# Layer norm spread over the steps of a two-block feed-forward kernel, and half of the second block's tiles normalised on ScalarE

## The chip, the cores and the metric

The kernel runs on one core of a Trainium2 chip. The metric is the device time in microseconds (us), the median over the runs shown. A profile of one execution shows what each engine did: PE is TensorE (PEld its weight loads), DVE is VectorE, ACT is ScalarE, POOL is GpSimd, SP is SyncE, which issues the large DMAs.

## What is computed

1024 tokens of width 256, float32. Two residual blocks, each behind a layer norm without weights:

```python
def _layernorm(x, axis=-1, eps=1e-05):
    m = jnp.mean(x, axis=axis, keepdims=True)
    v = jnp.var(x, axis=axis, keepdims=True)
    return (x - m) / jnp.sqrt(v + eps)
...
# block 1: 4 experts, the expert of a token follows from its id
for e in range(E):
    g = jax.nn.silu(jnp.einsum('bsd,fd->bsf', hidden_states, Wg[e]))
    u = jnp.einsum('bsd,fd->bsf', hidden_states, Wu[e])
    y = jnp.einsum('bsf,df->bsd', g * u, Wd[e])
    out = jnp.where((expert_ids == e)[..., None], y, out)
...
# block 2: 8 experts, the best two by score, weighed by a softmax
for e in range(E):
    h = jax.nn.silu(jnp.einsum('btd,hd->bth', x, W1[e])) * jnp.einsum('btd,hd->bth', x, W2[e])
    y = y + w[..., e:e + 1] * jnp.einsum('bth,dh->btd', h, W3[e])
...
x = x + _L0_xattn_ref(_layernorm(x, axis=-1), itok_BxS_13_99985, ctx_2048, ctx_2048, ctx_2048)
x = x + _L0_ffn_ref(_layernorm(x, axis=-1), L0_ffn_Wg, L0_ffn_W1, L0_ffn_W2, L0_ffn_W3)
```

In block 1 the three weights are the same tensor, so gate and up product are one.

## The kernel before

The tokens are two halves of 512 (h = 0, 1), each of four tiles of 128 tokens. The experts' hidden rows are cut into chunks of 128: 8 chunks in block 1 (b = 0), 11 in block 2 (b = 1). A **step** q is one chunk for one half: q 0 to 7 are block 1 of half 0, 8 to 15 block 1 of half 1, 16 to 26 block 2 of half 0, 27 to 37 block 2 of half 1. Every float32 product is made of three matmuls in a reduced format, from a high part and a low part of each operand (`w_hi`, `w_lo`, `hT_hi`, `hT_lo`, `act_hi`, `act_lo`).

All engines run the same list of steps, each in its own order, and wait on semaphores only:

- TensorE (`up`, `down`): `up(q)`, the product with the tokens into a PSUM bank `z` (6 matmuls of 512 columns in block 1, 12 in block 2), then the stages of slot 0, then `down(q-3)` (12 matmuls of 256 columns into `y`), then the stages of slot 1. `down` waits for `act_lo` of its step; a later `up` waits for earlier `act` results.
- ScalarE: `silu(q)` from `z` (L380), then `act_hi(q-1)` (L352), then this step's stages, then `w_hi` of a weight piece (L327).
- GpSimd: in block 1 `gated` = silu x gate (L315), then `rstd` (L285, a power of -0.5), then `w_lo` of a weight piece (L275). In block 2 only the last two.
- VectorE: in block 2 `gated` (L528); `act_lo(q-1)` (L503); `act(q)` (L538); `w_lo` of three pieces of block 1 (L509); then this step's stages, in the order residual sum, statistics, normalise (L436), tokens_lo (L443), router.

A **stage** stands in the table `STAGES`, which has three entries, for three **ways**: the layer norm of block 1 for half 1 (way (0,1), steps counted from 0), that of block 2 for half 0 (way (1,0), counted from 8) and for half 1 (way (1,1), counted from 16). The chain of a way is: statistics on VectorE, `rstd` on GpSimd, `norm` (4 tiles of 128x256) on VectorE, eight transposes on TensorE (`transpose_tokens`, L585), `tokens_hi` (L336) on ScalarE, `tokens_lo` on VectorE. TensorE waits inside its queue for each tile of `norm` that is late. In block 2 the router's scores, the best two and the softmax follow, and their gates (`gate_rows`, L492) are transposed at the end of step 16 and 26. `SPLIT_AT` says in which step a weight piece is split into `w_hi` and `w_lo`. The pieces come by DMA through a ring of 5 buffers.

Of the kernel before, what the change touches and what calls it, by code (L numbers as in the profile page):

```python
# [37 lines left out]
P = 128  # L38
# [18 lines left out]
BUFFERS = 3  # L57

RING = 5

# [15 lines left out]
    "statistics": (None, 2, 3),  # L76
    "inverse_deviation": (1, 4, 5),
    "normalise": (1, 4, 4),
    "transpose_tokens": ((4, 0), (6, 0), (6, 1)),
    "tokens_hi": (4, 5, 6),  # L80
    "tokens_lo": (5, 5, 5),
    "scores": (None, (7, 0), (7, 0)),
# [11 lines left out]
SPLIT_AT = {c - 3: (0, c) for c in range(FIRST_PIECES, CHUNKS[0])}  # L94
SPLIT_AT |= {6 + 2 * c: (1, c) for c in range(4)}
SPLIT_AT |= {FIRST[1, 0] + c - 5: (1, c) for c in range(4, CHUNKS[1])}
# [20 lines left out]
def ffn_moe(nc, x, token_ids, weights1, weights2, router, consts, out):  # L117
# [4 lines left out]
    with ctx:  # L122
# [35 lines left out]
        var = sb("var", [P, TILES])  # L158
        rstd = sb("rstd", [P, TILES])
        minus_half = sb("minus_half", [P, TILES])  # L160
        score_part = sb("score_part", [P, HALF_TILES, EXPERTS2])
# [22 lines left out]
        var_done, rstd_done = sem("var_done"), sem("rstd_done")  # L184
        norm_done, norm_T = sem("norm_done"), sem("norm_T")
        hT_hi_done, hT_lo_done = sem("hT_hi_done"), sem("hT_lo_done")
        scored, score_rows_done, scores_T = sem("scored"), sem("score_rows_done"), sem("scores_T")
# [83 lines left out]
        def _(pool):  # L271
# [6 lines left out]
            def inverse_deviation(b, h):  # L278

                for part, (n, tiles) in enumerate(LN_PARTS):  # L280
                    if n == ln_no(b, h):
# [4 lines left out]
                            .then_inc(rstd_done, 1)  # L286


            nc.gpsimd.memset(minus_half[:], -0.5).then_inc(reached_done, 1)
# [15 lines left out]
            for q, (b, h, c) in enumerate(STEPS):  # L305
                if b == 0:
# [5 lines left out]
                    if c == 0:  # L312
# [3 lines left out]
                        .then_inc(gated_done, 1)  # L316
                for way in due("inverse_deviation", q):
                    inverse_deviation(*way)
                if q in SPLIT_AT and SPLIT_AT[q] not in VECTOR_LO:
# [3 lines left out]
        def _(act_e):  # L323
# [5 lines left out]
            def tokens_hi(b, h):  # L329
                for k in range(KD):  # L330

                    act_e.wait_ge(norm_T, KD * ln_no(b, h) + k + 1)
                    if b == 1 and k == 0:

                        act_e.wait_ge(up_done, LAST[0, h] + 1)
                    nc.scalar.copy(hT_hi[:, h, k, :], y[h][k][:]).then_inc(hT_hi_done, 1)  # L336

            def gates_out(b, h):
# [35 lines left out]
            for q, (b, h, c) in enumerate(STEPS):  # L374
# [24 lines left out]
                if q in SPLIT_AT:  # L399
                    weight_hi(*SPLIT_AT[q])  # L400
            round_act(NSTEPS - 1)

        @block.vector
        def _(dve):
# [8 lines left out]
            def statistics(b, h, src):  # L413

                for n, tiles in LN_PARTS:
                    if n == ln_no(b, h):
# [8 lines left out]
                        link(last)  # L425
                        cols = slice(tiles.start, tiles.stop)
                        nc.vector.tensor_scalar(var[:, cols], mv[:, cols, 1], EPS, None, ALU.add).then_inc(var_done, 1)

            def normalise(b, h, src):
                if ln_no(b, h):  # L430

                    dve.wait_ge(norm_T, KD * ln_no(b, h))
                for i, t in enumerate(tiles_of(h)):

                    dve.wait_ge(rstd_done, ln_part_no(ln_no(b, h), t))
                    nc.vector.tensor_scalar(norm[:, i, :], src[:, t, :], mv[:, t, 0:1], rstd[:, t:t + 1],  # L436
                                            ALU.subtract, ALU.mult).then_inc(norm_done, 1)
# [82 lines left out]
            for q, (b, h, c) in enumerate(STEPS):  # L520
# [31 lines left out]
                for bb, hh in due("normalise", q):  # L552
                    normalise(bb, hh, (x_sb, x2_sb)[bb])
                for way in due("tokens_lo", q):
# [17 lines left out]
        def _(pe):  # L572
# [7 lines left out]
            def transpose_tokens(b, h):  # L580
                for k in range(KD):
                    for i in range(HALF_TILES):

                        pe.wait_ge(norm_done, HALF_TILES * ln_no(b, h) + i + 1)
                        last = nc.tensor.transpose(y[h][k][:, i * P:(i + 1) * P], norm[:, i, k * P:(k + 1) * P], ident)  # L585
# [146 lines left out]
```

## Time and profile before

| | us |
|---|---|
| median of 3 runs | 166.16 |
| the runs | 165.45, 166.16, 166.22 |
| span of the profiled execution | 165.1 |
| TensorE busy | 154.5 (94%) |
| VectorE busy | 114.8 (70%) |
| ScalarE busy | 65.1 (39%) |
| GpSimd busy | 55.9 (34%) |

TensorE is busy nearly throughout, so its remaining idle stretches, and the stretches in which its clock was granted at less than full speed, are where time is to be found. An engine's share of busy time includes time in which a running instruction was held up.

### The profile page before, as it was taken

The page shows a single profiled execution, that of the slowest core. Times are in us where ns is not written, and L with a number is a line of the kernel's source. Part 1 is how long each engine was busy: PE and PEld are TensorE (multiplying, and loading weights), DVE is VectorE, ACT ScalarE, POOL GpSimd, SP SyncE. Part 2 cuts the span into 40 slices and gives each one's busy share as a digit, 9 for nine tenths or more (in the row PEclk, how much of TensorE's full clock was granted, in tenths as well). Part 3 has the DMA queues.
Part 4 walks back from the last instruction along what each step waited for, and adds up shares of the span by engine and source line. Part 5 has one row for each costly group of instructions (what it writes and reads, how often), then busy time and mean ns, then how long its engine had stood idle before and what let it go on. Part 6 is the DMA issues. An engine that isn't in the chain of part 4 may idle for free.

```text
span 165.1 us, 2425 instructions
## 1 busy us (share of the span) xinstructions
PE 154.5 (94%) x892; PEld 131.7 (80%) x892; DVE 114.8 (70%) x225; ACT 65.1 (39%) x115; POOL 55.9 (34%) x47
## 2 busy tenths in 40 slices
PE   7599799999995999999999999999999999999991
PEld 2177689898982879888888778898888888888890
DVE  0788999955989865799999784945444744444452
ACT  3395557643742431763344432206222222222210
POOL 0599825779796330757464000000000000000000
PEclk9999999999999599999999999999999999999999
DMA  3975325232033000150000000000000300000003
GB/s 104 331 271 173 95 67 142 81 95 81 22 95 95 0 0 4 16 175 0 0 0 4 2 0 0 2 4 0 0 0 0 126 5 0 0 0 4 0 2 127
DMA packets 4332, 8.76 MB, mean 53 GB/s; under 512 B 736, under 2 KB 864, under 8 KB 4320
## 3 DMA queue, kind: packets, MB, share of 16 engines
q1 hardware_dynamic: 4176, 8.60, 16.7%
q8 instruction: 7, 0.11, 0.3%
q14 instruction: 5, 0.04, 0.1%
q10 hardware_dynamic: 144, 0.00, 0.0%
HBM read 7.55 MB, written 1.05 MB: 52 GB/s over the span
## 4 chain that ended last, share of the span: by engine, by line
PE 46%; DVE 17%; issue 14%; POOL 13%; ACT 4%; DMA 3%; SPq 1%; DVEq 0%; POOLq 0%; ACTq 0%
PE z L626 26%; PE y L651 18%; POOL gated L315 9%; DVE act L538 4%; DVE act_lo L503 4%; POOL w_lo L275 3%; DMA raw<-weights_dram 3%; DVE norm L436 2%; DVE x_sb L449 2%; DVE stats L421 2%; DVE gated L528 2%; ACT act_hi L352 1%; ACT w_hi L327 1%; PE y L585 1%; POOL rstd L285 1%
## 5 line engine op out<-in xcount | busy, mean ns | idle before, releaser
L626 PE MATMUL z<-hT_hi,w_hi 128*128 128x512 f32 x120 | 48.0, 400 | 0.6 <-ACT hT_hi L336 0.3
L626 PE MATMUL z<-hT_hi,w_lo 128*128 128x512 f32 x120 | 47.4, 395 | 0.0
L503 DVE TENSOR_TENSOR act_lo<-act,act_hi 128x512 fp32r<-128x512 f32 x38 | 33.4, 880 | 15.0 <-ACT act_hi L352 14.4
L651 PE MATMUL y<-w_hi,act_lo 128*128 128x256 f32 x152 | 43.5, 286 | 0.2 <-DVE act_lo L503 0.2
L651 PE MATMUL y<-w_hi,act_hi 128*128 128x256 f32 x152 | 43.5, 286 | 0.0
L651 PE MATMUL y<-w_lo,act_hi 128*128 128x256 f32 x152 | 43.4, 286 | 0.0
L380 ACT ACTIVATE silu<-z 128x512 f32<-128x512 f32 x38 | 22.7, 597 | 45.2 <-PE z L626 45.2
L626 PE MATMUL z<-hT_lo,w_hi 128*128 128x512 f32 x120 | 37.2, 391 | 0.0
L275 POOL TENSOR_TENSOR w_lo<-raw,w_hi 128x768 fp32r<-128x768 f32 (+1 forms) x15 | 27.4, 1839 | 19.3 <-ACT w_hi L327 19.3
L352 ACT CAST act_hi<-act 128x512 fp32r<-128x512 f32 x38 | 23.5, 618 | 26.0 <-DVE act L538 25.6
L651 PEld LDWEIGHTS y<-w_hi,act_lo 128*128 128x128 f32 x152 | 29.4, 193 | 2.1 <-issue 0.4
L651 PEld LDWEIGHTS y<-w_lo,act_hi 128*128 128x128 f32 x152 | 29.4, 194 | 1.2
L528 DVE TENSOR_TENSOR gated<-gate,z 128x512 f32<-128x512 f32 x22 | 15.0, 683 | 21.3 <-PE z L626 19.6
L651 PEld LDWEIGHTS y<-w_hi,act_hi 128*128 128x128 f32 x152 | 29.5, 194 | 0.0
L626 PEld LDWEIGHTS z<-hT_lo,w_hi 128*128 128x128 f32 x120 | 22.6, 188 | 5.3 <-DVE hT_lo L443 0.3
L626 PEld LDWEIGHTS z<-hT_hi,w_hi 128*128 128x128 f32 x120 | 22.9, 191 | 4.6 <-issue 0.9
L315 POOL TENSOR_TENSOR gated<-silu,gate 128x512 f32<-128x512 f32 x16 | 23.0, 1451 | 10.6 <-ACT silu L380 10.6
L626 PEld LDWEIGHTS z<-hT_hi,w_lo 128*128 128x128 f32 x120 | 22.9, 191 | 3.7
L538 DVE TENSOR_TENSOR act<-gated,silu 128x512 f32<-128x512 f32 x22 | 18.3, 833 | 0.0
L327 ACT CAST w_hi<-raw 128x768 fp32r<-128x768 f32 (+1 forms) x19 | 14.0, 742 | 4.4 <-DMA raw<-weights_dram 4.4
L538 DVE TENSOR_TENSOR act<-gated,z 128x512 f32<-128x512 f32 x16 | 10.9, 678 | 2.4 <-POOL gated L315 2.4
L436 DVE TENSOR_SCALAR norm<-x_sb,mv,rstd 128x256 f32<-128x256 f32 x16 | 10.4, 704 | 0.3 <-POOL rstd L285 0.3
(48 smaller groups left out, 75.3 us busy)
## 6 DMA issues: line engine op xcount, KB each, us to landing
raw<-weights_dram SPq DMA_DIRECT2D x11, 384.0 KB, 3.2
raw<-weights_dram SPq DMA_DIRECT2D x8, 256.0 KB, 4.8
x_sb<-x_dram SPq DMA_DIRECT2D x4, 256.0 KB, 4.6
out_dram<-x_sb SPq DMA_DIRECT2D x4, 256.0 KB, 2.5
consts_sb<-consts_dram SPq DMA_DIRECT2D x1, 68.0 KB, 3.8
ids_sb<-token_ids_dram ACTq DMA_DIRECT2D x1, 4.0 KB, 4.0
router_raw<-router_dram SPq DMA_DIRECT2D x1, 8.0 KB, 2.8
```

The costliest lines, as they stand in the source:

```text
L275: nc.gpsimd.tensor_tensor(w_lo[b][:, c, :], raw_piece(b, c), w_hi[b][:, c, :].bitcast(F32), ALU.subtract).then_inc(w_lo_pool, 1)
L315: nc.gpsimd.tensor_tensor(gated[:, q % BUFFERS, :], silu[:, q % BUFFERS, :], gate[:, h, :], ALU.mult)\
L327: nc.scalar.copy(w_hi[b][:, c, :], raw_piece(b, c)).then_inc(w_hi_done, 1)
L352: nc.scalar.copy(act_hi[:, q % BUFFERS, :], act[:, q % BUFFERS, :]).then_inc(act_hi_done, 1)
L380: nc.scalar.activation(silu[:, q % BUFFERS, :], z_banks(q)[0][:], ACT.Silu).then_inc(silu_done, 1)
L421: last = nc.vector.bn_stats(stats[:, t, :], src[:, t, :])
L436: nc.vector.tensor_scalar(norm[:, i, :], src[:, t, :], mv[:, t, 0:1], rstd[:, t:t + 1], ALU.subtract, ALU.mult).then_inc(norm_done, 1)
L503: nc.vector.tensor_tensor(act_lo[:, i, :], act[:, i, :], act_hi[:, i, :].bitcast(F32), ALU.subtract)\
L528: nc.vector.tensor_tensor(gated[:, i, :], gate[:, h, :], z_banks(q)[1][:], ALU.mult)\
L538: nc.vector.tensor_tensor(act[:, i, :], gated[:, i, :], factor, ALU.mult).then_inc(act_done, 1)
L626: return nc.tensor.matmul(bank[:], w[b][:, c, cols], tokens[:, h, k, :], **flags)
L651: last = nc.tensor.matmul(o, a[:, q % BUFFERS, rows], w[b][:, c, wd], start=(first and j == 0), stop=(c == CHUNKS[b] - 1 and j == 2), skip ...
```

## The change

Three things are changed.

- **Block 1, half 1.** The four `norm` tiles, which VectorE wrote one behind the other in step 1, are written one in each of the steps 1 to 4, each at the end of its step. The transposes move from slot 0 of step 4 to slot 0 of step 5, `tokens_hi` from step 4 to 5 and `tokens_lo` from step 5 to 6.
- **Block 2, half 0.** `rstd` and `norm` move from step 12 to step 11. `w_hi` and `w_lo` of piece (1,3) move from step 12 to step 14. The places of the other stages are as before.
- **Both halves of block 2.** VectorE writes two `norm` tiles; ScalarE writes the other two as `rstd * x + shift`. For that VectorE writes `minus_mean` (128x4) with the statistics, and GpSimd `shift = minus_mean * rstd` (128x2). In half 1 `rstd` moves from step 21 to 20; `norm` stays in step 20. ScalarE's two tiles come at the end of its step 11 (step 20 in half 1) and wait for `shift`.

```diff
@@ -56,6 +56,9 @@
 LAG = 3
 BUFFERS = 3
 
+
+DVE_TILES = 2
+
 RING = 5
 
 WARM = 12
@@ -74,11 +77,11 @@
 STAGES = {
     "sum": (None, 1, 2),
     "statistics": (None, 2, 3),
-    "inverse_deviation": (1, 4, 5),
-    "normalise": (1, 4, 4),
-    "transpose_tokens": ((4, 0), (6, 0), (6, 1)),
-    "tokens_hi": (4, 5, 6),
-    "tokens_lo": (5, 5, 5),
+    "inverse_deviation": (1, 3, 4),
+    "normalise": (None, 3, 4),
+    "transpose_tokens": ((5, 0), (6, 0), (6, 1)),
+    "tokens_hi": (5, 5, 6),
+    "tokens_lo": (6, 5, 5),
     "scores": (None, (7, 0), (7, 0)),
     "score_rows": (None, 7, 7),
     "transpose_scores": (None, (7, 1), (7, 1)),
@@ -92,7 +95,7 @@
 
 FIRST_PIECES = 4
 SPLIT_AT = {c - 3: (0, c) for c in range(FIRST_PIECES, CHUNKS[0])}
-SPLIT_AT |= {6 + 2 * c: (1, c) for c in range(4)}
+SPLIT_AT |= {(6, 8, 10, 14)[c]: (1, c) for c in range(4)}
 SPLIT_AT |= {FIRST[1, 0] + c - 5: (1, c) for c in range(4, CHUNKS[1])}
 
 VECTOR_LO = ((0, 0), (0, 5), (0, 6), (0, 7))
@@ -157,6 +160,8 @@
         mv = sb("mv", [P, TILES, 2])
         var = sb("var", [P, TILES])
         rstd = sb("rstd", [P, TILES])
+        shift = sb("shift", [P, TILES])
+        minus_mean = sb("minus_mean", [P, TILES])
         minus_half = sb("minus_half", [P, TILES])
         score_part = sb("score_part", [P, HALF_TILES, EXPERTS2])
         score = sb("score", [P, HALF_TILES, EXPERTS2])
@@ -183,6 +188,7 @@
         gate_T, gate_done = sem("gate_T"), sem("gate_done")
         var_done, rstd_done = sem("var_done"), sem("rstd_done")
         norm_done, norm_T = sem("norm_done"), sem("norm_T")
+        shift_done, norm_act = sem("shift_done"), sem("norm_act")
         hT_hi_done, hT_lo_done = sem("hT_hi_done"), sem("hT_lo_done")
         scored, score_rows_done, scores_T = sem("scored"), sem("score_rows_done"), sem("scores_T")
         gap_done, th_done = sem("gap_done"), sem("th_done")
@@ -285,6 +291,12 @@
                         nc.gpsimd.tensor_tensor(rstd[:, cols], var[:, cols], minus_half[:, cols], ALU.pow)\
                             .then_inc(rstd_done, 1)
 
+            def scaled_mean(h):
+
+                pool.wait_ge(rstd_done, ln_part_no(ln_no(1, h), h * HALF_TILES))
+                cols = slice(h * HALF_TILES + DVE_TILES, (h + 1) * HALF_TILES)
+                nc.gpsimd.tensor_tensor(shift[:, cols], minus_mean[:, cols], rstd[:, cols], ALU.mult).then_inc(shift_done, 1)
+
 
             nc.gpsimd.memset(minus_half[:], -0.5).then_inc(reached_done, 1)
             nc.gpsimd.memset(reached[:, 0, :], 1.0).then_inc(reached_done, 1)
@@ -314,8 +326,10 @@
                         pool.wait_ge(gate_done, ln_no(b, h) + 1)
                     nc.gpsimd.tensor_tensor(gated[:, q % BUFFERS, :], silu[:, q % BUFFERS, :], gate[:, h, :], ALU.mult)\
                         .then_inc(gated_done, 1)
-                for way in due("inverse_deviation", q):
-                    inverse_deviation(*way)
+                for bb, hh in due("inverse_deviation", q):
+                    inverse_deviation(bb, hh)
+                    if bb == 1:
+                        scaled_mean(hh)
                 if q in SPLIT_AT and SPLIT_AT[q] not in VECTOR_LO:
                     weight_lo(*SPLIT_AT[q])
 
@@ -334,6 +348,16 @@
 
                         act_e.wait_ge(up_done, LAST[0, h] + 1)
                     nc.scalar.copy(hT_hi[:, h, k, :], y[h][k][:]).then_inc(hT_hi_done, 1)
+
+            def normalise_rest(h):
+                act_e.wait_ge(shift_done, h + 1)
+                act_e.wait_ge(rstd_done, ln_part_no(ln_no(1, h), h * HALF_TILES))
+
+                act_e.wait_ge(norm_T, KD * ln_no(1, h))
+                for i in range(DVE_TILES, HALF_TILES):
+                    t = h * HALF_TILES + i
+                    nc.scalar.activation(norm[:, i, :], x2_sb[:, t, :], ACT.Identity, bias=shift[:, t:t + 1],
+                                         scale=rstd[:, t:t + 1]).then_inc(norm_act, 1)
 
             def gates_out(b, h):
 
@@ -398,6 +422,8 @@
                     gates_out(*way)
                 if q in SPLIT_AT:
                     weight_hi(*SPLIT_AT[q])
+                for _, hh in due("normalise", q):
+                    normalise_rest(hh)
             round_act(NSTEPS - 1)
 
         @block.vector
@@ -424,13 +450,15 @@
                             last = nc.vector.bn_aggr(mv[:, t, :], stats[:, t, :])
                         link(last)
                         cols = slice(tiles.start, tiles.stop)
+                        if b == 1:
+                            nc.vector.tensor_scalar(minus_mean[:, cols], mv[:, cols, 0], -1.0, None, ALU.mult)
                         nc.vector.tensor_scalar(var[:, cols], mv[:, cols, 1], EPS, None, ALU.add).then_inc(var_done, 1)
 
-            def normalise(b, h, src):
+            def normalise(b, h, src, parts=range(HALF_TILES)):
                 if ln_no(b, h):
 
                     dve.wait_ge(norm_T, KD * ln_no(b, h))
-                for i, t in enumerate(tiles_of(h)):
+                for i, t in [(i, h * HALF_TILES + i) for i in parts]:
 
                     dve.wait_ge(rstd_done, ln_part_no(ln_no(b, h), t))
                     nc.vector.tensor_scalar(norm[:, i, :], src[:, t, :], mv[:, t, 0:1], rstd[:, t:t + 1],
@@ -550,7 +578,10 @@
                     dve.wait_ge(x2_done, 2 * hh + 2)
                     statistics(1, hh, x2_sb)
                 for bb, hh in due("normalise", q):
-                    normalise(bb, hh, (x_sb, x2_sb)[bb])
+                    normalise(bb, hh, x2_sb, range(DVE_TILES))
+                if 1 <= q <= HALF_TILES:
+
+                    normalise(0, 1, x_sb, (q - 1,))
                 for way in due("tokens_lo", q):
                     tokens_lo(*way)
                 for _, hh in due("best_two", q):
@@ -581,7 +612,12 @@
                 for k in range(KD):
                     for i in range(HALF_TILES):
 
-                        pe.wait_ge(norm_done, HALF_TILES * ln_no(b, h) + i + 1)
+                        if b == 0:
+                            pe.wait_ge(norm_done, HALF_TILES * h + i + 1)
+                        elif i < DVE_TILES:
+                            pe.wait_ge(norm_done, 2 * HALF_TILES + DVE_TILES * h + i + 1)
+                        else:
+                            pe.wait_ge(norm_act, (HALF_TILES - DVE_TILES) * h + i - DVE_TILES + 1)
                         last = nc.tensor.transpose(y[h][k][:, i * P:(i + 1) * P], norm[:, i, k * P:(k + 1) * P], ident)
                     last.then_inc(norm_T, 1)
```

VectorE's queue, steps 1 to 4: `act_lo` (of the step before), `act`, `w_lo` (a weight piece) and `norm`. Before:

```order
L503 TENSOR_TENSOR act_lo<-act,act_hi 128x512 [waits act_hi_done]
L538 TENSOR_TENSOR act<-gated,z 128x512 [waits gated_done]
L436 TENSOR_SCALAR norm<-x_sb,mv,rstd 128x256 [waits rstd_done,norm_T]
L436 TENSOR_SCALAR norm<-x_sb,mv,rstd 128x256 [waits rstd_done] x3
L503 TENSOR_TENSOR act_lo<-act,act_hi 128x512 [waits act_hi_done]
L538 TENSOR_TENSOR act<-gated,z 128x512 [waits gated_done]
L509 TENSOR_TENSOR w_lo<-raw,w_hi 128x512 [waits w_hi_done]
```

And with the change, from the third of these `act_lo` on (steps 3 and 4):

```order
L531 TENSOR_TENSOR act_lo<-act,act_hi 128x512 [waits act_hi_done]
L566 TENSOR_TENSOR act<-gated,z 128x512 [waits gated_done]
L537 TENSOR_TENSOR w_lo<-raw,w_hi 128x512 [waits w_hi_done]
L464 TENSOR_SCALAR norm<-x_sb,mv,rstd 128x256 [waits rstd_done,norm_T]
L531 TENSOR_TENSOR act_lo<-act,act_hi 128x512 [waits down_done,act_hi_done]
L566 TENSOR_TENSOR act<-gated,z 128x512 [waits gated_done]
L537 TENSOR_TENSOR w_lo<-raw,w_hi 128x512 [waits w_hi_done]
L464 TENSOR_SCALAR norm<-x_sb,mv,rstd 128x256 [waits rstd_done,norm_T]
```

The last `norm` tile now stands behind nine other instructions of VectorE that it stood ahead of.

TensorE's queue, end of `up(5)` and the transposes of block 1's half 1, with the change (before, they stood behind `up(4)`, ahead of `down(1)`):

```order
L662 MATMUL z<-hT_hi,w_hi 128x512 [waits act_done,w_lo_vector]
L662 MATMUL z<-hT_hi,w_lo 128x512
L662 MATMUL z<-hT_hi,w_hi 128x512
L662 MATMUL z<-hT_hi,w_lo 128x512
L662 MATMUL z<-hT_lo,w_hi 128x512 x2
L621 MATMUL y<-consts_sb,norm 128x128 [waits norm_done,gate_done]
L621 MATMUL y<-consts_sb,norm 128x128 [waits norm_done] x7
L687 MATMUL y<-w_hi,act_lo 128x256 [waits act_lo_done]
```

They moved back by one `down` and one `up`: `down(2)` now stands behind them.

GpSimd's queue, steps 10 to 15. Before (`rstd` and `w_lo` of piece (1,3) are the fourth and fifth row):

```order
L315 TENSOR_TENSOR gated<-silu,gate 128x512 [waits act_done,silu_done] x2
L275 TENSOR_TENSOR w_lo<-raw,w_hi 128x768 [waits w_hi_done]
L315 TENSOR_TENSOR gated<-silu,gate 128x512 [waits act_done,silu_done] x2
L285 TENSOR_TENSOR rstd<-var,minus_half 128x4 [waits var_done]
L275 TENSOR_TENSOR w_lo<-raw,w_hi 128x768 [waits w_hi_done]
L315 TENSOR_TENSOR gated<-silu,gate 128x512 [waits act_done,silu_done] x3
```

And with the change:

```order
L281 TENSOR_TENSOR w_lo<-raw,w_hi 128x768 [waits w_hi_done]
L327 TENSOR_TENSOR gated<-silu,gate 128x512 [waits act_done,silu_done]
L291 TENSOR_TENSOR rstd<-var,minus_half 128x4 [waits var_done]
L298 TENSOR_TENSOR shift<-minus_mean,rstd 128x2 [waits rstd_done]
L327 TENSOR_TENSOR gated<-silu,gate 128x512 [waits act_done,silu_done] x3
L281 TENSOR_TENSOR w_lo<-raw,w_hi 128x768 [waits w_hi_done]
L327 TENSOR_TENSOR gated<-silu,gate 128x512 [waits act_done,silu_done]
```

`rstd` moved ahead of one `gated`, and `w_lo` of piece (1,3) from ahead of three `gated` to between the last two (those of steps 14 and 15).

## Rows read from the trace of the kernel before

**Rows 1.** The page: VectorE and others' busy time, and TensorE's granted clock in 40 slices
```profile
PE 154.5 (94%) x892; PEld 131.7 (80%) x892; DVE 114.8 (70%) x225; ACT 65.1 (39%) x115; POOL 55.9 (34%) x47
...
PEclk9999999999999599999999999999999999999999
```

**Rows 2.** Timeline, TensorE, step 4: start us, us busy, instruction, [idle before, releaser]
```profile
19.26 0.38 PE L585 MATMUL y<-consts_sb,norm 128*128 128x128 f32 x2
20.51 1.09 PE L585 MATMUL y<-consts_sb,norm 128*128 128x128 f32 x6 [0.88 <-DVE norm L436]
...
24.36 0.28 PE L651 MATMUL y<-w_hi,act_lo 128*128 128x256 f32 x1
```

**Rows 3.** Timeline, TensorE, the transposes of block 2's halves
```profile
51.03 0.30 PE L585 MATMUL y<-consts_sb,norm 128*128 128x128 f32 x1 [1.09 <-DVE norm L436]
52.21 1.41 PE L585 MATMUL y<-consts_sb,norm 128*128 128x128 f32 x7 [0.88 <-DVE norm L436]
53.38 0.36 PE L651 MATMUL y<-w_hi,act_lo 128*128 128x256 f32 x1
...
90.88 1.04 PE L585 MATMUL y<-consts_sb,norm 128*128 128x128 f32 x8
```

**Rows 4.** The chain that ended last, merged: start us, us, what
```profile
53.62 2.39 PE y L651 x12
56.02 1.96 PE z L626 x6
...
63.61 1.43 PE y L651 x12
...
111.16 2.75 PE z L626 x12
```

**Rows 5.** Timeline, VectorE, steps 1 to 4
```profile
16.73 4.05 DVE L436 TENSOR_SCALAR norm<-x_sb,mv,rstd 128x256 f32<-128x256 f32 x4
...
22.67 0.69 DVE L503 TENSOR_TENSOR act_lo<-act,act_hi 128x512 fp32r<-128x512 f32 x1
...
26.69 0.68 DVE L509 TENSOR_TENSOR w_lo<-raw,w_hi 128x512 fp32r<-128x512 f32 x1
```

**Rows 6.** Timeline, GpSimd, the same stretch
```profile
17.54 1.35 POOL L315 TENSOR_TENSOR gated<-silu,gate 128x512 f32<-128x512 f32 x1
19.04 1.26 POOL L315 TENSOR_TENSOR gated<-silu,gate 128x512 f32<-128x512 f32 x1 [0.15 <-ACT silu L380]
...
26.68 3.54 POOL L315 TENSOR_TENSOR gated<-silu,gate 128x512 f32<-128x512 f32 x2 [1.66 <-ACT silu L380]
```

**Rows 7.** Line L436 by stretch: ns min/median/max, starts (first and second tile, last)
```profile
L436 DVE TENSOR_SCALAR norm<-x_sb,mv,rstd x2: 1008/1196/1385, 16.7 to 17.7; 128x256 f32<-128x256 f32 x2
...
L436 DVE TENSOR_SCALAR norm<-x_sb,mv,rstd x1: 401/401/401, 20.4 to 20.4; 128x256 f32<-128x256 f32 x1
```

**Rows 8.** Timeline, GpSimd and VectorE side by side in block 2
```profile
79.53 1.85 POOL L275 TENSOR_TENSOR w_lo<-raw,w_hi 128x768 fp32r<-128x768 f32 x1 [2.02 <-ACT w_hi L327]
...
79.78 2.15 DVE L503 TENSOR_TENSOR act_lo<-act,act_hi 128x512 fp32r<-128x512 f32 x1
```

**Rows 9.** Groups by line, ScalarE: instruction xcount | busy us, mean ns | idle before
```profile
L352 ACT CAST act_hi<-act 128x512 fp32r<-128x512 f32 x38 | 23.5, 618 | 26.0 <-DVE act L538 25.6
...
L396 ACT ACTIVATE th<-gap 128x4 f32<-128x4 f32 x2 | 0.4, 205 | 6.2 <-DVE gap L471 6.2
```

**Rows 10.** Timeline, GpSimd, step 12 and step 15
```profile
47.92 1.00 POOL L285 TENSOR_TENSOR rstd<-var,minus_half 128x4 f32<-128x4 f32 x1
...
58.69 1.29 POOL L315 TENSOR_TENSOR gated<-silu,gate 128x512 f32<-128x512 f32 x1 [2.53 <-ACT silu L380]
```

**Rows 11.** Timeline, VectorE then TensorE, from act(15) to the gates' transposes
```profile
60.45 0.68 DVE L538 TENSOR_TENSOR act<-gated,z 128x512 f32<-128x512 f32 x1
...
63.91 0.63 DVE L492 COPY gate_rows<-w_tok 128x128 f32<-128x128 f32 x4
...
64.88 0.60 PE L577 MATMUL y<-consts_sb,gate_rows 128*128 128x128 f32 x4
```

## The prediction

> **What bounds the kernel now.** The page comes first: TensorE is busy 94% of the span, and in one of 40 slices, the fourteenth (53.7 to 57.8 us), its granted clock is about half [rows 1]. So the kernel gets shorter where TensorE waits or runs slowly, and nowhere else. The timeline of TensorE then gives the places. In step 4 it has done two transposes of block 1's half 1 when it waits 0.88 us for VectorE's `norm` [rows 2]. In step 14, at the transposes of block 2's half 0, it waits 1.09 and 0.88 us [rows 3]. The transposes of half 1 wait for nothing: eight take 1.04 us [rows 3]. The rest of the span is nearly free of idle time on TensorE but for the start and the end.
>
> What these places cost. Step 4: from the first transpose to the last 20.51 + 1.09 - 19.26 = 2.34, against 1.04: **1.3 us**. Step 14: TensorE came at 51.03 - 1.09 = 49.94, and was done at 52.21 + 1.41 = 53.62, against 50.98: 2.6, with the usual overlap of neighbours some **2.7 us**. Behind that idle stretch the clock fell to its lower level (1.2 GHz): `down(11)` took 2.39 us where the same 12 matmuls take 1.43, and the 6 of `up(15)` 1.96 where 12 take 2.75, so 6 about 1.38 [rows 4]. That is 0.96 + 0.58, some **1.6 us**. All three together are 5.6 us, 3.4% of the span.
>
> Why `norm` is late there: not by its own work. The last of the four tiles in step 1 took 0.40 us, the first 1.01 and the second 1.39 [rows 7]. The second started at 17.7 and ended at 19.05, just behind GpSimd's `gated`, 17.54 to 18.89 [rows 6]; four tiles took 4.05 [rows 5]. The same shows with two-input instructions of VectorE: `act_lo` started at 79.78 and ended at 81.93, while `w_lo` on GpSimd ran from 79.53 to 81.38, so it ended 0.55 behind it, where it takes 0.69 alone [rows 5, 8]. It goes the other way too: two `gated` took 3.54 against 1.26 for one [rows 6], 1.0 too much. So where an instruction of VectorE that reads SBUF twice (or a `norm` tile) meets one of GpSimd, the later one waits for the whole of the earlier.
> The Trainium skill (SBUF — State Buffer, "SBUF: two separate sides") says so of the pair of ports that the two engines share: an exclusive lock, held for the instruction. The trace agrees (2.15 us beside 1.85). If the two shared bandwidth instead, the walk below would be shorter by its held-up time and the sum would be that of the first rival.
>
> **The change, part by part.**
>
> *Block 1, half 1: one `norm` tile a step.* The first tile runs as before, 16.73 to 17.74. `down(1)` no longer stands behind the transposes, only behind `act_lo(1)`. That now meets `gated(2)` and ends at 18.89 + 0.55 = 19.44, so `down(1)` starts at 19.5, not at 21.4; `up(5)` waits a little for `w_lo` of piece 5 and is over at about 22.8. There the transposes stand, and they need the fourth tile. It stands behind `act_lo`, `act` and `w_lo` of steps 2 to 4: nine instructions of 0.6 us each from start to start (0.69 less the overlap) and three tiles of 0.33. Free of hold-ups the fourth tile would start at 16.73 + 9 x 0.60 + 3 x 0.33 = 23.1 and end at 23.5. Hold-ups, from the rows of the same pairs: first tile against `w_lo` 0.6; `act_lo(1)` against `gated(2)` 1.1; `w_lo` against `gated(3)` 0.8; against `gated(4)` 0.6; against `gated(5)` 0.7. Sum 3.8: the fourth tile ends at 27.3. A cross-check: before, the same 13 instructions in another order took from 16.73 to 26.69 + 0.68 = 27.37 [rows 5]. The total hardly changes, but the tile that TensorE needs was third from the front and is now the last.
> So TensorE comes at 22.8 and stands until 27.3, but for one transpose when the third tile comes (about 24.4); four or five more transposes take 0.6, and `down(2)` starts at 27.9 instead of 24.36 [rows 2]. This is net of the 1.3 us stall that goes: **+3.5 us**. Bounds: -0.2 (nothing held up: 23.5 + 0.6 against 24.36) and +4.2. I take 3.5, because the cross-check sits on it.
>
> *The clock there.* 4 us with three transposes is longer and emptier than the 3.1 us with one or two in step 14, behind which the clock fell [rows 3]. So it probably falls here. Price: 0 to 1.6, as in step 14; if it falls, **+1.3**, since part of the slow stretch can lie in the idle time itself.
>
> *Does the lateness last?* ScalarE's `tokens_hi` now stands in front of `silu(6)`, and waits for the transposes; `gated`, `w_lo` and `act` of steps 6 to 11 come some 1.5 us later than before, but TensorE comes 3.5 later, so it meets no new wait; it was continuously busy from step 5 to 13 and stays so. `tokens_lo` in step 6 is ready within half a microsecond of where `up(8)` needs it. Taken at nothing; at worst 0.5.
>
> *Block 2, half 0.* `rstd` ran at 47.92 to 48.92 [rows 10] and now runs one `gated` (1.3) earlier relative to its neighbours. With the lateness of 1.5 it ends near 48.7, `shift` (a 128x2 product) near 49.0, VectorE's two tiles near 49.5. ScalarE's two tiles are in no row; the 128x512 copies take 0.62 and a 128x4 0.2 [rows 9], so 0.2 to 0.6 each, I take 0.5 (near the larger, as they are long instructions): done near 50.1. TensorE comes at 49.8 + 3.5 = 53.3. Three microseconds of slack, so the wait goes and with it the fall of the clock: **-2.7 - 1.6 = -4.3 us**. It would have gone even with four tiles on VectorE. Of the 4.3 the bounds are 2.7 (the clock falls all the same) and 4.3.
> The Trainium skill (ScalarE: Activation LUTs, "What ACT_TABLE_LOAD costs") gives 186 ns, 93 more for each per-partition operand, and 0.833 ns an element: by it a tile would be an estimated 0.59 us. No row here shows it, and with 3 us of slack the sum stays the same.
>
> *`w_lo` of piece (1,3) between `gated(14)` and `gated(15)`.* Before, `gated(15)` ran at 58.69 as soon as silu was there [rows 10], `act(15)` at 60.45, and the gates' last row was ready at 64.54, just before TensorE wanted it at 64.88 [rows 11]. Now GpSimd is in `w_lo` (1.85 [rows 8], held up by `act_lo(13)` to 2.3) when silu(15) comes: it is free 1.5 later and held up again by `act_lo(14)` (0.5). In the new clock of events, without a fall of TensorE's clock, `act(15)` starts at 60.9, the gates' rows are ready 64.54 - 60.45 = 4.1 later at 65.0, and TensorE, which has gained, is there at 63.9 + 0.2: **+0.9 us**. Bounds 0 and 1.5.
>
> *Block 2, half 1.* `rstd` and `shift` go ahead of one `w_lo`, so VectorE's `var` is no longer held up, but that `w_lo` now meets `act` and the tiles, and ends where it did. The transposes waited for nothing before. Taken at nothing, bounds -0.4 and +0.4. The added `minus_mean`, 128x4, is under 0.1 and hidden by that slack; `shift` (twice) too.
>
> **Sum** against the profiled execution: 165.1 + 3.5 + 1.3 - 4.3 + 0.9 = 166.5. The median of the runs is 1.06 above the span, so **167.5 us**, +1.3.
>
> **The rivals.**
> 1. *The stall in step 5 is short.* The queues fall so that VectorE is seldom held up, the fourth tile is ready at 23.5 to 25.5, the clock stays up. For it: each hold-up depends on tenths of a microsecond. Against it: the cross-check. Time: 166.2 + (-0.2 to +1.7) - 4.3 + 0.9 = 162.6 to 164.5. Chance 0.18.
> 2. *The stall is as said, but the clock doesn't fall.* For it: the idle time of step 4 before, 0.9 us, brought no fall. Then 167.5 - 1.3 = 166.2 (165.4 to 166.7). Chance 0.25.
> 3. *Slower by more*, decided by whether the slow clock lasts on. If the clock falls in step 5 and again at the gates of step 16, where TensorE waits 0.9, or if the stretch at the lower clock is twice as long, 1.6 more: 169.0. It decides from the point where idle time at step 16 passes that of step 14 before. Chance 0.10.
> Forecast as said, 166.7 to 168.4: chance 0.47.
>
> **Range and chances.** 164.8 to 168.4: it leaves out rival 3 and the lower part of rival 1, 2 in 10. The forecast and rival 2 alone would give 165.4 to 168.4. A measurement of this kernel can tell 0.5% (0.83 us) from no change. Faster by more than that, under 165.33: all of rival 1 and a small part of 2, 0.20. Slower, over 166.99: most of the forecast's 0.47 and rival 3, 0.50. Between: 0.30.
>
> **What would show it.** In the changed kernel's timeline: the transposes of block 1's half 1 start near 22.8, with idle time before the last of them until about 27.3, and `down(2)` starts at 27.9. If they end before 25, rival 1 holds. The granted clock shows half in a slice near 26 to 32 us, or else rival 2 holds. The transposes in step 14 show no idle time before them and no half clock behind; if they do, the -4.3 is wrong. The gates' transposes in step 16 wait for `gate_rows` by about 0.9. I'd be wrong above all if VectorE's order of waiting and GpSimd's differ from the walk, since its five hold-ups carry the sum.

## The result: slower, 1.027 times

The changed kernel takes 170.87 us in the median of five runs, the kernel before 166.22 in its five: the ratio is 1.027, 95% interval 1.021 to 1.033. The forecast had the sign, 167.5 us, but the time lies outside the stated range of 164.8 to 168.4. The profiled execution has a span of 167.8 us and belongs to the run of 169.58; three of the other runs have spans of 169.0 to 169.1 and a lower mean clock (0.976 to 0.979 of full speed instead of 0.99). The fifth, 174.44 us at 0.959, is left out of the ratio, as every run is that lies over 1.5% above the fastest of its kernel. Time less span is 1.8 us in every run of every kernel whose span is known.

The page of the changed kernel, totals and granted clock, to be set beside [rows 1]:

```profile
PE 154.3 (92%) x892; PEld 131.4 (78%) x892; DVE 112.6 (67%) x223; ACT 67.1 (40%) x119; POOL 58.1 (35%) x49
...
PEclk9959999999999999999999999999999999999999
```

The slice with half clock is now the third, at the first transposes of the program, and no longer the fourteenth. The timeline of TensorE, at the places of the prediction (start us, us, instruction, [idle before, releaser]):

```profile
8.86 1.81 PE L621 MATMUL y<-consts_sb,norm 128*128 128x128 f32 x8
...
20.53 0.39 PE L687 MATMUL y<-w_hi,act_lo 128*128 128x256 f32 x1 [0.17 <-DVE act_lo L531]
...
23.72 0.38 PE L621 MATMUL y<-consts_sb,norm 128*128 128x128 f32 x2
25.18 0.33 PE L621 MATMUL y<-consts_sb,norm 128*128 128x128 f32 x1 [1.07 <-DVE norm L464]
27.77 0.77 PE L621 MATMUL y<-consts_sb,norm 128*128 128x128 f32 x5 [2.27 <-DVE norm L464]
28.30 0.36 PE L687 MATMUL y<-w_hi,act_lo 128*128 128x256 f32 x1
...
54.16 1.03 PE L621 MATMUL y<-consts_sb,norm 128*128 128x128 f32 x8
...
55.86 0.39 PE L687 MATMUL y<-w_hi,act_lo 128*128 128x256 f32 x1 [0.66 <-DVE act_lo L531]
...
59.63 0.64 PE L631 MATMUL y<-hT_hi,router_hl 128*16 128x512 f32 x2 [0.69 <-DVE hT_lo L471]
...
67.63 0.73 PE L608 MATMUL y<-consts_sb,gate_rows 128*128 128x128 f32 x4 [0.62 <-DVE gate_rows L520]
```

How to read it beside [rows 2, 3, 11]. The stall of step 4 (0.88 idle) has become one of 1.07 and 2.27 in step 5. The stall of step 14 is gone: eight transposes in 1.03, as half 1 had them before. Behind it stand three waits that were not there: `down(11)` for `act_lo`, the router's scores for `hT_lo`, the gates' transposes for `gate_rows`.

TensorE's groups come in the same order in both kernels but for the one that moved. The difference of their starts, changed kernel less the one before, shows where time comes and goes. The second column of numbers is from another execution of the changed kernel, `after_again`, told of below:

| TensorE's group | changed kernel | its other execution | what happened since the row above |
|---|---|---|---|
| `down(0)` | +0.95 | +0.02 | half clock at the first transposes, in one of the two |
| `down(2)` | +3.94 | +3.48 | the stall of step 5 |
| `down(4)` | +4.02 | +4.37 | half clock behind it, in the other of the two |
| `down(5)`, behind `up(8)` | +4.42 | +4.78 | `up(8)` waits 0.4 for `hT_lo` |
| `up(14)` | +4.38 | +4.75 | nothing in 15 us |
| `up(15)` | +1.58 | +1.94 | stall and half clock of step 14 gone, `down(11)` waits |
| scores of half 0 | +1.82 | +2.18 | wait for `hT_lo` |
| `down(13)` | +1.97 | +2.32 | |
| `up(17)` | +2.90 | +3.27 | wait for `gate_rows` |
| `up(22)` | +2.50 | +2.89 | the 0.22 us wait of before gone |
| scores of half 1, and on to the end | +2.69 | +3.08 | the tokens come no earlier |

### The profile page after: what moved, and what is told of

Its sections match the earlier page's. It is cut to its first block, busy times and chain, and to the rows that moved or that the text cites. A ratio compares the mean times of both kernels' runs of the same rounds, so it can differ in the third digit from the quotient of the medians.

```text
span 167.8 us, 2434 instructions
## 1 busy us (share of the span) xinstructions
PE 154.3 (92%) x892; PEld 131.4 (78%) x892; DVE 112.6 (67%) x223; ACT 67.1 (40%) x119; POOL 58.1 (35%) x49
## 3 DMA queue, kind: packets, MB, share of 16 engines
HBM read 7.55 MB, written 1.05 MB: 51 GB/s over the span
## 4 chain that ended last, share of the span: by engine, by line
PE 47%; DVE 29%; issue 8%; ACT 6%; POOL 4%; DMA 3%; SPq 1%; ACTq 0%; DVEq 0%; POOLq 0%
PE z L662 26%; PE y L687 18%; DVE act L566 8%; DVE act_lo L531 6%; DMA raw<-weights_dram 3%; DVE norm L464 2%; DVE stats L447 2%; ACT act_hi L376 2%; DVE w_lo L537 2%; DVE hT_lo L471 2%; POOL gated L327 2%; PE y L621 1%; POOL w_lo L281 1%; ACT hT_hi L350 1%; DVE x_sb L477 1%
## 5 line engine op out<-in xcount | busy, mean ns | idle before, releaser
L531 DVE TENSOR_TENSOR act_lo<-act,act_hi 128x512 fp32r<-128x512 f32 x38 | 34.5, 907 | 18.8 <-ACT act_hi L376 18.6
L687 PE MATMUL y<-w_hi,act_hi 128*128 128x256 f32 x152 | 43.0, 283 | 0.0
L281 POOL TENSOR_TENSOR w_lo<-raw,w_hi 128x768 fp32r<-128x768 f32 (+1 forms) x15 | 28.3, 1895 | 13.0 <-ACT w_hi L341 12.8
L687 PEld LDWEIGHTS y<-w_hi,act_hi 128*128 128x128 f32 x152 | 29.0, 191 | 0.0
L566 DVE TENSOR_TENSOR act<-gated,silu 128x512 f32<-128x512 f32 x22 | 20.0, 907 | 0.0
L621 PE MATMUL y<-consts_sb,norm 128*128 128x128 f32 x32 | 5.4, 310 | 3.3 <-DVE norm L464 3.3
```

Source lines behind the costliest of these rows:

```text
L281: nc.gpsimd.tensor_tensor(w_lo[b][:, c, :], raw_piece(b, c), w_hi[b][:, c, :].bitcast(F32), ALU.subtract).then_inc(w_lo_pool, 1)
L531: nc.vector.tensor_tensor(act_lo[:, i, :], act[:, i, :], act_hi[:, i, :].bitcast(F32), ALU.subtract)\
L566: nc.vector.tensor_tensor(act[:, i, :], gated[:, i, :], factor, ALU.mult).then_inc(act_done, 1)
L687: last = nc.tensor.matmul(o, a[:, q % BUFFERS, rows], w[b][:, c, wd], start=(first and j == 0), stop=(c == CHUNKS[b] - 1 and j == 2), skip ...
```

## The experiments

Each is described by its edit. They were run in three groups, each beside the kernel before on the same chip; it had medians of 166.7 to 166.9. TensorE's mean granted clock differs between executions of one kernel, and the time with it, so where it matters below the spans of executions at full clock throughout are compared too. The kernel before had 12 of these in its 67 runs of the three groups, with spans of 163.2 to 163.6.

### Block 1's part alone

```diff
 STAGES = {
-    "normalise": (1, 4, 4),
-    "transpose_tokens": ((4, 0), (6, 0), (6, 1)),
-    "tokens_hi": (4, 5, 6),
-    "tokens_lo": (5, 5, 5),
+    "normalise": (None, 4, 4),
+    "transpose_tokens": ((5, 0), (6, 0), (6, 1)),
+    "tokens_hi": (5, 5, 6),
+    "tokens_lo": (6, 5, 5),
...
+                if 1 <= q <= HALF_TILES:
+                    normalise(0, 1, x_sb, (q - 1,))
```

> The kernel before with the block 1 part of the change alone: one norm tile a step in steps 1 to 4, transposes in step 5. Theory 1 (the fourth tile is last in VectorE's queue and TensorE stands for it): the transposes of step 5 wait 3 to 3.5 us in sum and down(2) comes 3.1 us later than before; the wait in step 14 shrinks from 2.7 to about 1, since TensorE comes 3 later and the others 1.5 later, and the clock falls in step 5 instead of behind step 14. Sum 166.2 + 3.3 + 0.4 - 1.7 - 1.6 + (0 to 1.6) = 166.6 to 168.2. Rival (block 1's part is harmless, the loss lies in block 2's part): 166.2 - 1.3 = 164.9 or less, no idle time above 1 us in step 5.

Measured: 173.45 us, ratio 1.039 (1.027 to 1.051), slower than the whole change. Its timelines, TensorE in step 14 and VectorE in step 9:

```profile
57.32 0.30 PE L587 MATMUL y<-consts_sb,norm 128*128 128x128 f32 x1 [1.05 <-DVE norm L436]
58.51 1.98 PE L587 MATMUL y<-consts_sb,norm 128*128 128x128 f32 x7 [0.88 <-DVE norm L436]
```

```profile
45.95 1.29 DVE L449 TENSOR_TENSOR x_sb<-y,x_sb 128x512 f32<-128x512 f32 x2 [0.42 <-PE y L653]
```

The stall of step 5 is there: relative to `down(0)`, `down(2)` comes 3.0 us later than in the kernel before, and half clock behind it adds 1.6. But the wait of step 14 is what it was in [rows 3], 1.05 and 0.88 us, though TensorE comes 6.3 us later. So the other engines are late by the same amount, not by 1.5: the residual sum in step 9 waits for TensorE's last `down` of half 0, and what follows (statistics, `rstd`, `norm`) is tied to it. The 6.3 us are 0.9 of half clock at the program's start, these 3.0 and 1.6, 0.4 at `up(8)` and 0.4 at `down(10)`, which waits for `act_lo`. Theory 1 holds for the stall, and the expectation failed where it let VectorE catch up.

### The place of the transposes alone

```diff
-    "transpose_tokens": ((4, 0), (6, 0), (6, 1)),
-    "tokens_hi": (4, 5, 6),
-    "tokens_lo": (5, 5, 5),
+    "transpose_tokens": ((5, 0), (6, 0), (6, 1)),
+    "tokens_hi": (5, 5, 6),
+    "tokens_lo": (6, 5, 5),
```

> The kernel before with the transposes of block 1's half 1 in step 5 (tokens_hi in step 5, tokens_lo in step 6), the four tiles still in step 1. If the place of the transposes alone costs something, it shows here; theory 1 (only the last tile's place does) expects no idle time at the transposes, down(1) later held only by act_lo(1): -0.5 to -1.3 against the kernel before up to step 13. Theory 1b (steps 9 to 13 are tied to TensorE, so what TensorE gains ahead of step 14 it waits for there) expects the gain to be lost at step 14 unless VectorE's part comes earlier too: the same time within 0.8.

Measured: 170.31 us, ratio 1.024 (1.016 to 1.032). Neither theory had it. TensorE:

```profile
21.95 0.39 PE L651 MATMUL y<-w_hi,act_lo 128*128 128x256 f32 x1 [1.96 <-DVE act_lo L503]
...
26.41 1.04 PE L585 MATMUL y<-consts_sb,norm 128*128 128x128 f32 x8
27.20 0.36 PE L651 MATMUL y<-w_hi,act_lo 128*128 128x256 f32 x1
```

With four tiles ahead of it in VectorE's queue, `act_lo(1)` is as late as before, and `down(1)` now waits 1.96 us for it. In the kernel before, the transposes lay in that wait. Now they come on top with 0.8 us, the clock falls behind the longer idle stretch (this costs 1.5, by the starts of the groups), and `up(8)` waits 0.4 for `hT_lo`. The transposes of step 4 were filling a wait.

### Two tiles a step instead of one

```diff
-                if 1 <= q <= HALF_TILES:
-                    normalise(0, 1, x_sb, (q - 1,))
+                if 1 <= q <= 2:
+                    normalise(0, 1, x_sb, (2 * q - 2, 2 * q - 1))
```

Once in the kernel with block 1's part alone, once in the changed kernel.

> ln1_only with two tiles in each of the steps 1 and 2 instead of one in each of 1 to 4. Theory 1: the last tile is ready near 22 instead of 27.4, the transposes of step 5 wait under 0.3, and against ln1_only the whole 6 us go: 165 to 166.5, at or below the kernel before. Rival (the later transposes or tokens_lo in step 6 cost as such): still over 168.

> The changed kernel with two tiles in each of the steps 1 and 2 instead of one in each of 1 to 4, nothing else changed. Theory 1: the 3.1 us of step 5 and the fall of the clock behind it go; what is left is block 2's part: 164.5 to 165.5, as ln2_only or 0.5 faster, and faster than the kernel before. Rival (the loss of the changed kernel is in block 2's part too): over 167.

Measured: 167.80 us, ratio 1.012 (1.007 to 1.017), for the first; 166.23, ratio 1.001 (0.998 to 1.005), for the second. TensorE, the first kernel:

```profile
22.90 1.04 PE L587 MATMUL y<-consts_sb,norm 128*128 128x128 f32 x8
...
32.08 1.10 PE L628 MATMUL z<-hT_lo,w_hi 128*128 128x512 f32 x2
...
51.65 0.30 PE L587 MATMUL y<-consts_sb,norm 128*128 128x128 f32 x1 [1.06 <-DVE norm L436]
```

The stall of step 5 is gone in both: the tile's place in VectorE's queue is its cause, and 4.6 us of the changed kernel's time (170.87 to 166.23; 4.3 by the two ratios) hang on it with the clock. But both times lie above what was expected, by 1.3 and 0.7 us, and block 1's part remains no gain: with it, 166.23; without it (the next experiment), 165.29. `up(8)` now waits 0.8 for `hT_lo`, whose step was moved from 5 to 6. In the first kernel `down(10)` waits another 0.4, and the wait of step 14 stays as it was.

### Block 2's part alone

The changed kernel with block 1's part undone:

```diff
-    "normalise": (None, 3, 4),
-    "transpose_tokens": ((5, 0), (6, 0), (6, 1)),
-    "tokens_hi": (5, 5, 6),
-    "tokens_lo": (6, 5, 5),
+    "normalise": (1, 3, 4),
+    "transpose_tokens": ((4, 0), (6, 0), (6, 1)),
+    "tokens_hi": (4, 5, 6),
+    "tokens_lo": (5, 5, 5),
...
```

> The changed kernel with the block 1 part undone (four norm tiles in step 1, transposes in step 4). Theory 2 (ScalarE stands for shift in step 11 and silu(12), act_hi(11) and tokens_hi come late): no wait at the transposes of step 14 but waits of down(11) for act_lo and of the scores for hT_lo of 1.5 to 3 us in sum: 166.2 - 4.3 + 0.9 + (1.5 to 3) = 164.3 to 165.8. Rival (ScalarE's wait costs nothing): 162.8.

Measured: 165.29 us, ratio 0.998 (0.994 to 1.003). TensorE, and ScalarE in step 11:

```profile
51.49 0.39 PE L685 MATMUL y<-w_hi,act_lo 128*128 128x256 f32 x1 [0.71 <-DVE act_lo L532]
...
55.27 0.64 PE L629 MATMUL y<-hT_hi,router_hl 128*16 128x512 f32 x2 [0.69 <-DVE hT_lo L472]
```

```profile
47.96 1.09 ACT L359 ACTIVATE norm<-x_sb,shift,rstd 128x256 f32<-128x256 f32 x2 [3.59 <-POOL shift L298]
```

ScalarE stands 3.59 us for `shift`. Queued behind it are `silu(12)`, whose z was ready, `act_hi(11)`, and through them `act_lo(11)` and the tokens. The two waits take back some 1.8 us of the gain, and the gates of step 16 another 0.9: together the 2.7 us of the wait that went. So at full clock this kernel has the span of the kernel before, 163.3 to 163.5 us. What block 2's part saves is only the half clock behind step 14, and the kernel before has that in some of its executions, not in all.

### ScalarE's tiles one step later in its queue

```diff
-                for bb, hh in due("normalise", q):
+                for bb, hh in due("normalise", q - 1 if q < FIRST[1, 0] else q):
                     if bb == 1:
                         normalise_rest(hh)
```

So the two tiles of half 0 stand behind `silu(12)` and `act_hi(11)`. Once in the kernel with block 2's part alone, once in the changed kernel.

> ln2_only with ScalarE's two tiles of block 2's half 0 behind silu(12) and act_hi(11) instead of ahead of them. Theory 2 (ScalarE stands for shift in step 11 and so act_lo(11) and the tokens come late): down(11) no longer waits, 0.5 to 1.5 less than ln2_only. Rival (the tiles themselves then come too late): idle time at the transposes of step 14, the same or slower.

> The changed kernel with ScalarE's two tiles of block 2's half 0 behind silu(12) and act_hi(11). Theory 2 (in the changed kernel too ScalarE's wait for shift is what makes act_lo(11) and the tokens late): down(11) waits no more for act_lo and the scores less for hT_lo, 1.0 to 1.5 less than the changed kernel, 169.4 to 170. Rival (something else makes them late): within 0.5 of it.

Measured: 163.97 us, ratio 0.987 (0.981 to 0.994), for the first, and 169.55, ratio 1.022 (1.013 to 1.031), for the second: 1.3 us less than their partners each. TensorE, the first kernel:

```profile
50.67 1.03 PE L619 MATMUL y<-consts_sb,norm 128*128 128x128 f32 x8
...
54.82 0.63 PE L629 MATMUL y<-hT_hi,router_hl 128*16 128x512 f32 x2 [0.29 <-DVE hT_lo L472]
...
62.82 0.73 PE L606 MATMUL y<-consts_sb,gate_rows 128*128 128x128 f32 x4 [0.64 <-DVE gate_rows L521]
```

And the second:

```profile
58.78 0.64 PE L631 MATMUL y<-hT_hi,router_hl 128*16 128x512 f32 x2 [0.27 <-DVE hT_lo L471]
```

In both the transposes still wait for nothing and `down(11)` no longer waits; the scores wait 0.29 and 0.27 instead of 0.69. Theory 2 holds in both kernels. The first is faster than both kernels of the case: 163.97 against 166.72 for the kernel before beside it, of which the spans at full clock (162.0 to 162.2 against 163.2 to 163.6) show 1.3 us; the rest is half clock that it has more seldom.

### The step alone, and the moved weight piece

`rstd` and `norm` of half 0 in step 11, all tiles on VectorE; then the same with the split of piece (1,3) in step 14:

```diff
-    "inverse_deviation": (1, 4, 5),
-    "normalise": (1, 4, 4),
+    "inverse_deviation": (1, 3, 5),
+    "normalise": (1, 3, 4),
...
-SPLIT_AT |= {6 + 2 * c: (1, c) for c in range(4)}
+SPLIT_AT |= {(6, 8, 10, 14)[c]: (1, c) for c in range(4)}
```

> The kernel before with rstd and the norm of block 2's half 0 in step 11 instead of 12, all four tiles on VectorE, w_lo of piece (1,3) still in step 12. By theory 2 the gain of step 14 comes without ScalarE: tiles done near 50.5, wait 0.7 instead of 2.7, no fall of the clock behind: 166.2 - 2.0 - 1.6 = 162.6, at most 164.2 if the clock falls all the same. Rival (the tiles are held up by gated(12) and w_lo as before): 165.5 to 166.2.

> The same with w_hi and w_lo of piece (1,3) moved to step 14, as in the change. If that move costs what the walk said (gates of step 16 late by 0.9) and the tiles gain 0.7: within 0.3 of early_only, with idle time of 0.5 to 1 before the gates' transposes of step 16. If w_lo in step 12 is what holds the tiles up: 1 to 2 us faster than early_only.

Measured: 166.82 us, ratio 1.002 (0.998 to 1.007), and 165.54, ratio 0.995 (0.991 to 0.999). The tiles on VectorE, the first kernel, then the second:

```profile
48.44 4.73 DVE L436 TENSOR_SCALAR norm<-x_sb,mv,rstd 128x256 f32<-128x256 f32 x4 [0.39 <-POOL rstd L285]
```

```profile
47.72 3.25 DVE L436 TENSOR_SCALAR norm<-x_sb,mv,rstd 128x256 f32<-128x256 f32 x4 [0.38 <-POOL rstd L285]
```

With `w_lo` of piece (1,3) in GpSimd's queue between `gated(12)` and `gated(13)`, four tiles take 4.73 us and the step earlier is worth nothing; with it away they take 3.25. So the moved split is a part of the gain, not just of the cost, and `early_only` missed its forecast of 162.6 because the tiles were held up as before. ScalarE's half is worth another 1.6 us, 163.97 against 165.54 (1.5 at full clock), where its place in the queue is right; some 0.2 of it comes in half 1, whose tiles and `rstd` differ too.

### The moved `w_lo` behind `gated(15)`

```diff
-                if q in SPLIT_AT and SPLIT_AT[q] not in VECTOR_LO:
+                if q == LAST[0, 1]:
+                    weight_lo(1, 3)
+                if q in SPLIT_AT and SPLIT_AT[q] not in VECTOR_LO + ((1, 3),):
                     weight_lo(*SPLIT_AT[q])
```

> rest12 with w_lo of piece (1,3) behind gated(15) instead of ahead of it. If that w_lo is what makes the gates of step 16 late, their wait of 0.64 goes and the time falls by 0.6 to 0.9, to 163.1 to 163.4. Rival (something else makes them late, or w_lo collides with the scores' chain): the same time.

> early_split14 (no work on ScalarE, norm in step 11) with w_lo of piece (1,3) behind gated(15). What ScalarE's half is worth shows against rest12_lo15: with theory 2, 0.3 to 1 us more than rest12_lo15, 163.5 to 164.5. If ScalarE's half is worth nothing: the same within 0.3.

Measured: 164.32 us, ratio 0.989 (0.985 to 0.993), and 165.65, ratio 0.998 (0.994 to 1.002): no change against their partners. GpSimd, VectorE and TensorE of the first:

```profile
56.75 1.82 POOL L281 TENSOR_TENSOR w_lo<-raw,w_hi 128x768 fp32r<-128x768 f32 x1
```

```profile
56.87 2.25 DVE L534 TENSOR_TENSOR act_lo<-act,act_hi 128x512 fp32r<-128x512 f32 x1 [0.69 <-ACT act_hi L378]
```

```profile
62.78 0.73 PE L608 MATMUL y<-consts_sb,gate_rows 128*128 128x128 f32 x4 [0.64 <-DVE gate_rows L523]
```

`gated(15)` is early now, but `w_lo` runs into `act_lo(14)`, holds it for 1.56 us more, and `act(15)` behind it starts where it did (59.04, against 59.06). Whether the gates would be in time with no `w_lo` near them is open: the runs without it in this place lack the gain that brings TensorE there early.

### The changed kernel once more

> The changed kernel once more, for a trace of an execution with its usual clock (its runs were near 170.9 with a granted clock of 0.978, the profiled one 169.58 with 0.99 and full clock behind step 5). If the clock falls behind the stall of step 5 in the usual run, this trace shows half clock near 28 to 33 us and some 1.5 us between down(2) and down(3) more than before; if it falls elsewhere, the offsets show where.

Measured: a span of 168.2 us (169.97 with what lies around it). The page's clock, and TensorE behind the stall of step 5:

```profile
PEclk9999996999999999999999999999999999999999
```

```profile
26.86 1.33 PE L621 MATMUL y<-consts_sb,norm 128*128 128x128 f32 x5 [2.27 <-DVE norm L464]
...
28.20 0.41 PE L687 MATMUL y<-w_lo,act_hi 128*128 128x256 f32 x1
```

Here the start is at full clock and the half clock (1.2 GHz; a matmul of 256 columns takes 0.41 instead of 0.28) follows the stall. By the offsets it costs 1.3 us: `down(5)` comes 4.76 later, relative to `down(0)`, against 3.47 in the execution shown first. The usual run, 169.1, is what both falls give together: 167.8 + 1.3, or 168.2 + 0.9. That the usual run has both is worked out from these sums and from its mean clock; it was not traced.

## Why the prediction missed

The forecast's 167.5 us and the 170.87 measured lie 3.4 us apart. Of these 1.7 belong to the term of step 14, which took no account of what waits behind ScalarE's tiles; 0.9 are the half clock at the program's start, which was no term; and 0.7 come from the step from span to time. Point by point, by the prediction's own terms; sizes from the offsets, relative to `down(0)`, and times less the 0.95 us by which `down(0)` is late, which is called the prediction's time scale.

- **The stall in step 5: held.** +3.5 was forecast, from the fourth tile ready at 27.3; it was ready at 26.8 on the prediction's time scale, and `down(2)` came 3.0 us later (3.5 with the fallen clock, in the other execution). The walk through the hold-ups carried: they came to 3.3 us, 3.8 were forecast. The row of the tile:

```profile
27.32 0.40 DVE L464 TENSOR_SCALAR norm<-x_sb,mv,rstd 128x256 f32<-128x256 f32 x1
```

- **The clock there: held in one of the two traces.** +1.3 forecast, +1.3 measured where it fell. The rival without the fall, 166.2, is ruled out by the sum, not by the clock: the execution shown first had no fall in step 5 and was still at 169.58.
- **Does the lateness last: the step that failed first.** "Come some 1.5 us later than before, but TensorE comes 3.5 later" let the other engines catch up. They don't: `var` of half 0 was ready 4.3 us later than before (50.55 against 46.21), as late as TensorE. This alone would have cost nothing in the sum, but it ate the slack: three microseconds were forecast, and ScalarE's tiles ended at 53.43, 0.7 us before TensorE came at 54.16; they were forecast for 50.1 and came at 52.5 on its time scale. `up(8)` waited 0.4 us, within the worst case of 0.5.
- **Step 14: the term that was mis-sized.** -4.3 was forecast and the wait and the half clock did go, but the net from `up(14)` to the scores was -2.6. The prediction looked only at when the tiles would be done, and asked nowhere what is queued behind ScalarE's wait. Two waits took their place, 0.9 and 0.85 us by the starts of the groups (0.66 and 0.69 as idle time in the rows): `down(11)` for `act_lo`, the scores for `hT_lo`. And the 1.6 us for the clock were read from one execution of the kernel before; others of its executions don't have them. ScalarE, then VectorE, in the changed kernel:

```profile
52.33 1.10 ACT L359 ACTIVATE norm<-x_sb,shift,rstd 128x256 f32<-128x256 f32 x2 [3.12 <-POOL shift L298]
...
53.81 0.60 ACT L376 CAST act_hi<-act 128x512 fp32r<-128x512 f32 x1
```

```profile
54.45 1.36 DVE L531 TENSOR_TENSOR act_lo<-act,act_hi 128x512 fp32r<-128x512 f32 x1 [1.58 <-ACT act_hi L376]
```

- **The gates of step 16: held in size.** +0.9 forecast, +0.93 measured. The cause given, `w_lo` ahead of `gated(15)`, is not shown: with it behind, the gates are as late, by another collision of the same instruction.
- **Block 2's half 1: held.** Nothing forecast, -0.4 and then +0.2 to 0.3 measured.
- **From span to time: a plain slip.** The prediction added 1.06 us, the difference of the profiled span and the median of the runs. The runs show 1.8 between a run's span and its own time: the profiled execution was one above the median. With 1.8 the sum would have given 168.3. And the half clock at the start, 0.9 us in the trace shown first and, by its time, in the usual run, was no term at all; it comes in 7 of the 11 traces of variants too (0.6 to 0.9 us), also where the start is that of the kernel before, so the change is not needed for it. Why it comes in one execution and not in another stays open.

In `after_again`, whose clock fell where the prediction had it, the sum was 166.5 us and the span 168.2: the 1.7 us between are the two waits behind ScalarE. The other differences cancel: 0.4 less for the stall with its clock, 0.4 more at `up(8)`.

The case for the first rival, a short stall, was counted at 0.18; nothing of it showed. The third, slower by more through the clock, named a mechanism that is part of the usual run's time, but not its place.

## What to carry to other kernels

When work is spread over the steps of a loop, look for the last piece and its reader: VectorE's work was the same and TensorE went on 3 us later, because the piece that TensorE waits for had become the last in VectorE's queue. A wait put into an in-order queue is paid by everything behind it, so an offloaded instruction belongs behind the engine's regular work of that step: the same two tiles, two instructions further back, gave 1.3 us and made the version that beats both (163.97 us). And a stage that looks as if it delayed TensorE may be filling a wait that is there anyway.

## What the runs showed of the hardware

- A `norm` tile of 128x256 on ScalarE, with scale and bias per partition, takes 0.59 us against 0.40 on VectorE alone. The prediction's estimate of 0.59 us, from the Trainium skill's 186 ns, 93 for each per-partition operand and 0.833 an element (ScalarE: Activation LUTs, "What ACT_TABLE_LOAD costs"), agrees with the trace. All four, ns min/median/max:

```profile
L359 ACT ACTIVATE norm<-x_sb,shift,rstd x4: 587/594/603, 52.3 to 89.8; 128x256 f32<-128x256 f32 x4
```

- VectorE and GpSimd held each other up in every trace here: four tiles took 4.73, 4.05 or 3.25 us by what GpSimd ran beside them, two on ScalarE took 1.09 to 1.10 each time. Moving `w_lo` out of the way of one instruction put it in the way of the next.
- The clock fell to its lower level behind idle stretches of 2 us (block 1's transposes moved alone, from 22.4 us on) and behind that of step 5 in one execution but not in another of the same kernel. In `early_only` it did not fall behind 0.93 and 0.94 us of idle time in step 14, where it fell in the kernel before behind 1.09 and 0.88. So it can be priced, 1.3 to 1.6 us a time within the program, but from one trace one can't say that it will or won't fall.
